# Another order of twelve row-major score groups in a fused attention and gated FFN kernel

## What is computed

```python
K = _split_heads(x @ Wk + bk, H)
V = _split_heads(x @ Wv + bv, H)
scores = jnp.einsum('bhqd,bhkd->bhqk', Q, K) + mask      # causal
attn = jax.nn.softmax(scores, axis=-1)
o = jnp.einsum('bhqk,bhkd->bhqd', attn, V)
x = _layernorm(x + (x + gelu(o) @ Wf + bf))
x = _layernorm(x + (silu(x @ wg.T) * (x @ wu.T)) @ wd.T)
```

## The kernel before

| burst | 0 | 1 | 2 | 3 | 4 | 5 | 6 | 7 |
|---|---|---|---|---|---|---|---|---|
| groups | t0 s0 t1 | s1 t2 s2 | t3 s3 t4 | s4 t5 s5 | t6 s6 t7 | s7 t8 s8 | t9 s9 t10 | s10 t11 s11 |

## Time and profile before

### The profile page before, as it was taken

One profiled execution on the slowest core, in us unless ns is written; L12 is line 12 of the kernel. 1 busy time (PEld: TensorE's weight loads), 2 busy tenths in 40 slices (PEclk: granted clock), 3 DMA queues, 4 the chain that ended last, 5 costly groups with the idle time before them and its releaser, 6 DMA issues. The chain is left out here.

```text
span 1997.3 us, 38522 instructions
## 1 busy us (share of the span) xinstructions
PE 1868.8 (94%) x10304; PEld 968.8 (49%) x10304; DVE 1535.2 (77%) x3597; ACT 1040.6 (52%) x1523; POOL 1139.4 (57%) x1200
## 2 busy tenths in 40 slices
PE   6799999999999999999999999878879999999996
PEld 5344444444444444444444444323337767767673
DVE  3887878888788878878788787767736887878874
ACT  2255555555655555555555555445544555655653
POOL 2177677677677677777777767766831221221212
PEclk9799999999999999999999999889989999999998
DMA  8844545554553545454464464383138666675610
GB/s 270 249 132 143 170 143 162 145 181 139 153 181 110 177 136 173 147 168 160 120 194 147 138 175 126 107 227 86 51 83 212 171 158 181 167 177 173 150 67 21
DMA packets 260962, 303.17 MB, mean 152 GB/s; under 512 B 28048, under 2 KB 177680, under 8 KB 260880
## 3 DMA queue, kind: packets, MB, share of 16 engines
q1 hardware_dynamic: 260880, 302.19, 52.5%
HBM read 174.20 MB, written 127.93 MB: 151 GB/s over the span
## 5 line engine op out<-in xcount | busy, mean ns | idle before, releaser
L936 ACT ACTIVATE weights<-ring 128x1024 f32<-128x1024 f32 (+3 forms) x768 | 601.3, 810 | 357.7 <-PE ring L684 355.2
L654 POOL TENSOR_TENSOR weight_sum<-weight_sum,weights 128x512 f32<-128x512 f32 (+3 forms) x448 | 682.9, 1524 | 9.7
L684 PE MATMUL o_acc<-weights,v_pair 128*64 128x512 f32 (+3 forms) x3072 | 619.4, 510 | 9.5 <-POOL weights L632 8.9
L632 POOL TENSOR_SCALAR_AFFINE_SELECT weights<-weights 128x256 f32<-128x256 f32 x512 | 224.5, 444 | 347.4 <-ACT weights L936 345.7
L1083 DVE TENSOR_REDUCE part_max<-ring 128x2 f32<-128x1024 f32 x256 | 300.2, 1214 | 104.0 <-PE ring L684 103.9
L684 PE MATMUL ring<-q_stack,k_stack 50*128 50x512 f32 (+3 forms) x1536 | 314.1, 414 | 55.2 <-DVE part_max L1083 29.3
L675 POOL TENSOR_TENSOR h_lo<-hidden,h_hi 128x512 f16<-128x512 f32 x96 | 114.5, 1194 | 399.4 <-ACT h_hi L905 399.4
L684 PE MATMUL ring<-k_stack,q_stack 48*128 48x512 f32 (+3 forms) x1536 | 307.3, 403 | 22.2 <-DMA k_stack<-k_rows 12.7
L1091 DVE CUSTOM_DVE_ANT_0 scrap<-ring,causal 128x128 bf16<-128x128 f32 (+3 forms) x512 | 229.3, 485 | 79.8 <-PE ring L684 79.3
L1091 DVE CUSTOM_DVE_ANT_0 scrap<-ring,causal,part_max 128x128 bf16<-128x128 f32 (+3 forms) x512 | 251.3, 547 | 49.6 <-PE ring L684 49.3
L684 PEld LDWEIGHTS o_acc<-weights,v_pair 128*64 128x64 f32 x3072 | 173.5, 137 | 229.9 <-issue 204.4
(11 more groups left out here) (105 smaller groups left out, 2153.5 us busy)
## 6 DMA issues: line engine op xcount, KB each, us to landing
v_pairs<-v_unit SPq DMA_DIRECT2D x64, 512.0 KB, 5.6
v_pair<-v_pairs SPq DMA_DIRECT2D x64, 512.0 KB, 5.5
o_heads<-o_pair SPq DMA_DIRECT2D x64, 512.0 KB, 5.3
g<-o_heads SPq DMA_DIRECT2D x16, 2048.0 KB, 8.2
den_wide<-reciprocals SPq DMA_DIRECT2D x32, 1024.0 KB, 13.4
q_stack<-q_rows SPq DMA_DIRECT2D x128, 192.0 KB, 3.5
k_stack<-k_rows SPq DMA_DIRECT2D x128, 192.0 KB, 4.2
q_rows<-x_hi SPq DMA_DIRECT2D x32, 512.0 KB, 5.1
```

What stands on the lines that cost most here:

```text
L632: pool.affine_select(out=diag, in_=diag, compare_op=ALU.is_ge, fill=0.0, base=0, pattern=[[0, 2], [1, P]], channel_multiplier=-1).then_inc ...
L654: pool.tensor_tensor(dst, other, W[t][:, :, :], ALU.add).then_inc(s_add, 1)
L684: return nc.tensor.matmul(o, l, r, start=start, stop=stop)
L936: nc.scalar.activation(W[t][:, :, :], bank_of("t", t)[:, :, 0:width_of(t)], ACT.Exp).then_inc(s_w, 1)
```

## The change

One table is permuted: the order in which the s groups are issued and read. Their number, their widths and their instructions are the same.

```diff
-GS = ((0, 0), (4, 0), (5, 0), (2, 0), (6, 0), (7, 0), (1, 0), (4, 1), (5, 1), (3, 0), (6, 1), (7, 1))
+GS = ((4, 0), (0, 0), (2, 0), (5, 0), (6, 0), (7, 0), (1, 0), (3, 0), (5, 1), (7, 1), (4, 1), (6, 1))
```

## The result

| | before | after |
|---|---|---|
| median of the runs beside each other | 1998.26 us | 2027.13 us |
| ratio, 95% interval | | 1.0133 (1.0098 to 1.0167) |
| profiled execution | 1999.08 us | 2028.52 us |
| its span, mean granted clock | 1997.3 us, 0.973 | 2026.8 us, 0.962 |

The change costs 29 us. I had forecast 1999.7 us in a range of 1989 to 2014, so the time lies outside the range.

What follows compares the result with a forecast made beforehand. TensorE, 94% busy, was taken as back to back except where VectorE holds it at two places in a round. Loop +8.1 and last pairs -6.8 gave +1.3 us on the profiled 1999.08: 2000.4, median 1999.7, range 1989 to 2014.

Steps and rivals of the forecast that it cites:

- Place A: Bursts 5 and 6, behind VectorE's second running add: a longer s7 delays t9 by 0.5 and t10 by 0.68 to 0.69 us.
- Place B: Burst 2, where t4 waits for s2 in three rounds of four: the stall of 0.6 us goes.
- t4's stall: Burst 2: t4 goes out about 1.0 us after t3 in place of 0.39; the stall was to go.
- The margin of t2: Burst 1: t2 must wait for a full s0, with 0.15 to 0.2 us to spare except in r%4=1.
- rival 1: The full group in burst 0 holds t2: 12 us over the sum, 2012, or 2020; chance 0.16.
- r%4=2 to 3: Transition between these rounds of the four-round pattern: no stall to recover, +0.53 us in full, 14 times.
- The last pairs: From round 57 on, without jobs beside the scores: five transitions gain 1.35 us each, -6.8 us (-2.5 to -11).
- One sign that the prediction had named as wrong: Cast and subtraction before s1 and s2: means other than 0.93 and 0.92 us would show the forecast wrong.
- Rival 2: Idle time moved to bursts 5 and 6 drops the clock in r%4=2 rounds: 1.8 us each, +25, 2025; chance 0.04.
- the size of the cycle: Four loop rounds: +0.53 us at r%4=2 to 3, +0.05 at r%4=0 to 1, about 0 at the other two.
- t11's wait: Burst 7: without burst 6's job, t11 waits for s9, which takes back 0.1 us; next t0 is +0.58.

Runs made afterwards that it cites:

- e1: The first seven places of the new order, s7 to s11 as in the kernel before: 1991.26 us, 0.9955 of before.
- e7: The new kernel with the second half of the x split moved from burst 4 to behind s8 in burst 5 (r%4=0 rounds): 2010.4 us, 1.0056 of before.
- e5: The kernel before with a third order: s6 to s8 light, the longest group at s3, s10 and s11 lighter: 1967.81 us, 0.9837 of before.
- e10: The kernel of e5 run once more, unchanged: 1966.10 us, 0.9826 of before.
- e6: e5 with the second half of the x split moved from burst 4 to behind s8 in burst 5: 1979.22 us, 0.989 of before.
- e8: The new kernel with s8 and s9 exchanged, so the 512-wide seeded group comes after s7: 2040.26 us, 1.0204 of before.
- e2: The last five places of the new order (s7 to s11), s0 to s6 as in the kernel before: 2022.25 us, 1.0104 of before.

## Why the prediction was wrong

**Right.** Both places and their direction. Place A: t9 was to move by 0.5 and t10 by 0.69; bursts 5 and 6 grew by 0.53 to 0.55 and by 0.15 in r%4=1, 2 and 3; in r%4=0, without a fall, bursts 4 and 5 together grew by 0.68 and burst 6 by nothing. Place B: t4's stall is gone everywhere. The margin of t2: it waits in r%4=1 alone, where it follows s1 0.67 us later than in the other rounds (0.6 worked out), so rival 1 fell in the new kernel, and e1 shows that it is real where the cast is caught until later. r%4=2 to 3 was the transition that gives nothing back. The last pairs are shorter, by 3.6 us where I took 6.8 (2.5 to 11).

One sign that the prediction had named as wrong showed beside the fall: the cast and the subtraction have other means than 0.93 and 0.92 us (the new kernel, 220 to 1236 us):

```profile
L1103 DVE CAST shift_parts<-rowmax 128x16 fp32r<-128x16 f32 x46 | 29.5, 642 | 2.1
L1107 DVE TENSOR_TENSOR shift_parts<-rowmax,shift_parts 128x16 fp32r<-128x16 f32 x46 | 22.6, 492 | 0.0
```

The cast does not end with the same add of GpSimd in every round, as was assumed: in r%4=2 it takes 0.18 us. This is why VectorE is 24 us less busy, and it left the sum as it was: over the four rounds bursts 0 to 2 became 1.66 us shorter, where 1.6 to 1.7 were worked out.

**Wrong: the clock, which the sum put at nothing.** Rival 2 named the mechanism, idle time at bursts 5 and 6, and priced a fall at 1.8 us (1.6 measured). I gave it 0.04, with the reason that "the trace shows no fall in the loop, with stalls of about the same length". That was the failing step. The stalls of r%4=0 before are 0.63 us at t9 and 0.45 at t4. t9 has no margin there, so the 0.68 us by which s7 grows come on top of the first: 0.63 + 0.68 is 1.31, against 0.74 for the longest single piece in the loop of before, and all idle pieces of the round together grow from 1.2 to 1.6 us. I put the falls into r%4=2, and they came in r%4=0. They are worth 14 of the 29 us: nine falls in the trace, and e7, which has none and is 16.7 us faster with rounds of nearly the same length.

**Wrong: the size of the cycle.** +0.6 us was forecast, +1.0 measured. The missing 0.4 is in burst 7. I credited the rounds with the 0.11 and 0.05 us by which s10 and s11 are narrower, and took too little of it back in r%4=1 and 3 (the text says 0.1 for t11's wait, but +0.53 to +0.58 is 0.05). Only r%4=2 has the credit (burst 7 shorter by 0.13). In r%4=1 and 3 t11 waits for the longer s9, so that bursts 6 and 7 together are 0.17 us longer. In r%4=0 job 1 waits for VectorE's split of job 0's result, which a narrower s10 on TensorE does not hasten. 13.5 times 0.4 is 5 us. With these the loop loses 13 us and not 8.

**Not forecast:** some 4 us ahead of round 3. The clock's first stretches at half rate end at 93 us there and at 85 before. No experiment ties that to the order. e5 and e10, the same kernel, start round 2 2.1 us apart, and e1, faster than the kernel before, starts round 3 at 109.0 us, where the new kernel does at 110.0 and the one before at 105.4. It stays open.

## What to carry to other kernels

Before a reordering, write down for each round of the pattern what TensorE will idle at each place, not only what the sum of waits does over the cycle: a wait that doubled in one round of four cost as much through the clock (14 us) as the longer cycle did (13). That the clock held before the change is little evidence that it holds after it; the rival needs its price, and a chance to go with it. If two halves of a change remove the same stall, only one of them is paid for; price each alone. And a tiny VectorE instruction beside a long GpSimd add is worth the add's remainder, so its start relative to that add is a thing to place: 0.4 us sooner at the start was 1.7 us sooner at the end.

## What the runs showed of the hardware

- *The clock fell behind idle pieces of a fraction of a microsecond to 1.6 us, and their length alone does not decide it.* All 31 falls between 100 and 1240 us, in six of the kernels, start 0.2 to 2.3 us after the end of an idle piece of 0.5 us or more (in the new kernel after 1.31 to 1.41 us ahead of t9). But e6 idles 1.61 us in one piece and 2.6 in sum in nine rounds and has one fall, while e8 has five falls in rounds with 0.35 and 0.78 us. In the new kernel itself round 16 has the long piece (1.31) and no fall; in rounds 12, 20 and 24 part of the wait lay at t7 in burst 4, t9's piece is 0.96 to 1.08 us, and the clock held. So that e7 has none cannot be put down to its shorter pieces alone. The Trainium skill, "TensorE: Matmul & The Clock Gate", section "HAM oscillation — how this bites in real kernels", has idle gaps between matmuls as the cause of such falls; the traces agree in that each fall comes behind such a gap.
- *The same idle piece brings a fall in one round and none in another.* In e2 t9 idles 1.30 or 1.31 us in each of rounds 20 to 48 with r%4=0. The falls of rounds 24, 28, 32 and 36 come 17.4, 17.8, 18.2 and 18.6 us after t0, and round 40 has none. These are t9's rows in rounds 36 and 40:

```profile
845.75 0.44 PE L684 MATMUL ring<-q_stack,k_stack 50*128 50x384 f32 x2 [1.31 <-DVE rowmax L1091]
...
934.01 0.44 PE L684 MATMUL ring<-q_stack,k_stack 50*128 50x384 f32 x2 [1.30 <-DVE rowmax L1091]
```

  What else decides was not varied by itself, nor was the moment at which the wait falls; it stays open.
- *VectorE and GpSimd hold each other up*, and the lengths say so: a cast of 16 columns takes between 0.16 and 1.89 us, a cast of 1024 columns 0.71 or 2.10, a subtraction of 1024 columns 1.22 or 2.12 (3.17 in e6). The Trainium skill, "SBUF — State Buffer", section "SBUF: two separate sides", states it as an exclusive lock, taken by the one that starts first; the traces agree in both directions. The caught instructions of 16 columns end within 0.04 us of GpSimd's add. The caught split of 1024 columns in e7 ends 1.09 us after the add, about its own length, and the mask of GpSimd behind it takes 1.39 us and not 0.41. The cast of 1024 columns in e5 ends 0.55 us after it.
